# Shaping the decoder's weights and bias inside the first block of a recurrent network with routed experts, and doing both halves of the first projection in a row

## What is computed

```python
xn = layernorm(x)
# branch 1: a recurrence over 2048 steps
x_sub = xn[:, ::2]; x_sub = x_sub * rsqrt(mean(x_sub**2) + eps) * g_norm
x_proj, gate = split(x_sub @ w_in.T + b_in)
h = tanh(h * A + x_proj[t][:, :, None] * Bm)      # for each step t, (4, 512, 64)
y = h @ Cm.sum(0) + Dv * x_proj[t]
s = (y * silu(gate)) @ w_out.T + b_out            # each row used twice
# branch 2: 8 experts, top 2
spikes = sigmoid(xn @ W_enc + b_enc); cont = spikes @ W_s2c + b_s2c
gate8 = normalized top-2 of softmax(cont @ Wr + br)
e_out = sum over experts of gate8 * (relu(cont @ W1 + b1) @ W2 + b2)
decoded = sigmoid(e_out @ W_c2s + b_c2s) @ W_dec + b_dec
g = silu(layernorm(decoded) * ln_g + ln_b)
out = x + s * g
```

## Time and profile before

| | |
|---|---|
| median of 3 runs | 5803.54 us (5798.73 to 5804.52) |
| profiled execution, own time | 5802.78 us |
| its span | 5801.0 us |
| PE busy | 5580.6 us (96%) |
| DVE busy | 5403.5 us (93%) |
| POOL busy | 5287.9 us (91%) |
| ACT busy | 4595.4 us (79%) |

### The profile page before, as it was taken

How to read it: one execution, slowest core, us unless ns; L and a number is a source line. 1 busy time by engine, 2 the same in 40 slices (tenths; PEclk the granted TensorE clock), 3 DMA queues, 4 the chain that set the end, 5 groups by cost and what they waited for, 6 DMA issues and landing times.

```text
span 5801.0 us, 88242 instructions
## 1 busy us (share of the span) xinstructions
PE 5580.6 (96%) x28770; PEld 3073.1 (53%) x28770; DVE 5403.5 (93%) x9108; ACT 4595.4 (79%) x9941; POOL 5287.9 (91%) x2828
## 2 busy tenths in 40 slices
PE   6999999999999999999999999999999999999998
PEld 3555555555555555555555555555555555555554
DVE  5999999999999999999999999999999999999997
ACT  5878878788788787887887878878878788788786
POOL 5999999999999999999999999999999999999997
PEclk9999999999999999999999999999999999999999
DMA  6454544544444445444454454444444444444443
GB/s 166 113 121 107 122 115 111 123 112 116 120 108 121 116 111 122 112 116 120 108 120 117 110 121 113 115 120 109 119 118 110 120 114 114 120 110 118 119 109 88
DMA packets 158222, 673.41 MB, mean 116 GB/s; under 512 B 45761, under 2 KB 46785, under 8 KB 92225
## 3 DMA queue, kind: packets, MB, share of 16 engines
q1 hardware_dynamic: 157762, 667.76, 48.0%
HBM read 617.26 MB, written 50.33 MB: 115 GB/s over the span
## 4 chain that ended last, share of the span: by engine, by line
PE 76%; ACT 14%; DVE 7%; issue 3%; SPq 1%; DMA 0%; POOL 0%; ACTq 0%; POOLq 0%
PE bank L973 17%; PE bank L921 15%; PE ps_y L887 11%; PE ps_acc L985 9%; PE bank L1037 8%; PE ps_acc L1037 8%; ACT h L598 4%; PE bank L908 4%; DVE ps_z L1144 4%; ACT conte L707 3%; DVE ps_z L1138 2%; ACT wide L718 1%; PE bank L1020 1%; PE ps_acc L1020 1%; PE bank L959 1%
## 5 line engine op out<-in xcount | busy, mean ns | idle before, releaser
L525 POOL TENSOR_TENSOR u<-xb,bt 128x1024 f32<-128x1024 f32 x2048 | 4811.0, 2360 | 387.1 <-DVE ps_z L1144 315.6
L598 ACT ACTIVATE h<-ps_z 128x512 f32<-128x512 f32 x4096 | 2408.0, 599 | 1008.3 <-DVE ps_z L1144 807.9
L1138 DVE TENSOR_TENSOR ps_z<-h,ps_A 128x512 f32<-128x512 f32 x4096 | 2664.7, 691 | 314.7 <-ACT h L598 233.1
L1144 DVE TENSOR_TENSOR ps_z<-ps_z,u 128x512 f32<-128x512 f32 x4096 | 2655.3, 691 | 0.0
L973 PE MATMUL bank<-wide,w 65*128 65x256 f32 x4096 | 1015.0, 393 | 18.5 <-ACT wide L718 18.5
L887 PE MATMUL ps_y<-h,c_wide 128*32 128x512 f32 x8192 | 962.0, 599 | 49.0 <-ACT h L598 49.0
L921 PE MATMUL bank<-xnT,w_enc 128*128 128x256 f32 x4096 | 901.3, 381 | 2.8 <-ACT wide L671 2.8
L973 PEld LDWEIGHTS bank<-wide,w 65*128 65x128 f32 x4096 | 730.6, 189 | 315.3 <-issue 152.6
L921 PEld LDWEIGHTS bank<-xnT,w_enc 128*128 128x128 f32 x4096 | 772.9, 190 | 158.9 <-issue 53.3
L887 PEld LDWEIGHTS ps_y<-h,c_wide 128*32 128x32 f32 x8192 | 227.2, 109 | 566.8 <-issue 418.1
L908 PE MATMUL bank<-w_in,xnT 128*128 128x512 f32 x1024 | 474.4, 606 | 7.6 <-DVE c_wide L1214 1.6
(11 more groups left out here) (124 smaller groups left out, 4285.1 us busy)
## 6 DMA issues: line engine op xcount, KB each, us to landing
xb<-x_proj_scratch SPq DMA_DIRECT2D x2048, 256.0 KB, 4.6
xbuf<-in_L_attn_x SPq DMA_DIRECT2D x256, 128.0 KB
xres<-in_L_attn_x SPq DMA_DIRECT2D x512, 64.0 KB
out<-g SPq DMA_DIRECT2D x256, 128.0 KB
x_proj_scratch<-xp SPq DMA_DIRECT2D x256, 64.0 KB
w_in<-in_L_attn_w_in SPq DMA_DIRECT2D x1, 2048.0 KB, 8.1
w_enc<-in_L_ffn_W_enc SPq DMA_DIRECT2D x1, 2048.0 KB, 16.5
w_dec<-in_L_ffn_W_dec SPq DMA_DIRECT2D x1, 2048.0 KB, 20.4
```

Of the source, the lines that this page charges most:

```text
L525: pool.tensor_tensor(u[:, tau % 2, :, :], xt, bt[:, :, :], ALU.mult).then_inc(u_ready, 1)
L598: act.activation(h[:, tau % RING, f, :], ps_z[:, f, :], ACT.Tanh).then_inc(h_ready, 1)
L1138: dve.tensor_tensor(ps_z[:, f, :], h[:, (tau - 1) % RING, f, :], ps_A[:, f, :], ALU.mult).then_inc(m_done, 1)
L1144: dve.tensor_tensor(ps_z[:, f, :], ps_z[:, f, :], u[:, tau % 2, f, :], ALU.add).then_inc(z_ready, 1)
```

## The change

The preamble is shortened. PE sums the columns of the weights as they are loaded; the factor of one half goes into the instructions that use the sums. Both `proj_in` groups run one after the other, and `gt` is made right after `xp`. The eight pieces of `w_dec` (and the small shift) move from the preamble into block 0 on ACT, at the slots 7.5, 8.5, ... 14.5. The bias `b_dec_all` takes four DVE instructions in block 0 in place of three in the preamble, at the slots 3, 4, 5 and 6. On DVE the long reduction for `w_dec_sum` comes behind the short ones for the router. New waits: the first decoding waits for the shaped weights, block 0's two seeds wait for steps of the bias, and in every block but the first `spikes` of bank 0 also waits until the second decoding of the block before is filled.

```diff
+ACT_SHAPE = (7.5, 8.5, 9.5, 10.5, 11.5, 12.5, 13.5, 14.5)
+DVE_SHAPE = (3.0, 4.0, 5.0, 6.0)
...
                 wait_filled(act, at)
+                if k == 0 and not is_first(blk):
+                    wait_dec_filled(act, blk - 1, 1)
                 drained(half_tanhs(bank[k % 2], k, b_enc_col), at)
...
+                if is_first(blk):
+                    act.wait_ge(biases_steps, 4)
                 act.activation(dec_out[q][:, :], b_dec_all[:, :], ACT.Copy).then_inc(dec_seeded, 1)
...
-                if not is_first(blk):
+                if is_first(blk):
+                    act.wait_ge(biases_steps, 1)
+                else:
                     wait_dec_drained(act, blk - 1, 1)
...
             proj_out(0, 0, 0)
+            proj_out(0, 0, 1)
             act.wait_ge(early_loaded, EARLY)
...
+            act.wait_ge(columns_summed, 1)
+            act.activation(cont_bias[0:M, :], ps_y[0:M, 0:1], ACT.Identity, scale=0.5, bias=cont_bias[0:M, :]
+                           ).then_inc(biases_shifted, 1)
+            act.activation(w_s2c[:, :, :], w_s2c[:, :, :], ACT.Copy, scale=0.5)
...
-            act.wait_ge(weights_shaped, 2)
-            for k in range(KH):
-                ins = act.activation(w_dec[:, k, :], w_dec[:, k, :], ACT.Identity, bias=w_dec_shift[:, k:k + 1], scale=0.5)
-            ins.then_inc(weights_shaped, 1)
...
-            proj_out(0, 0, 1)
+            def shape_decoder(k):
+                if k == 0:
+                    act.wait_ge(weights_shaped, 1)
+                    act.activation(w_dec_shift[:, :], w_dec_sum[:, :], ACT.Copy, scale=-0.5 / D).then_inc(weights_shaped, 1)
+                    act.wait_ge(weights_shaped, 2)
+                    act.wait_ge(columns_summed, 2)
+                ins = act.activation(w_dec[:, k, :], w_dec[:, k, :], ACT.Identity, bias=w_dec_shift[:, k:k + 1], scale=0.5)
+                if k == KH - 1:
+                    ins.then_inc(decoder_shaped, 1)
...
             proj_in(0, 0, 0)
-            pe.wait_ge(weights_shaped, 3)
+            proj_in(0, 0, 1)
+            pe.wait_ge(early_loaded, EARLY)
...
+            def shape_bias(n):
+                if n == 0:
+                    dve.wait_ge(columns_summed, 2)
+                    ins = dve.scalar_tensor_tensor(out=b_dec_all[:, :], in0=ps_acc[:, :], scalar=0.5, in1=b_dec_all[:, :],
+                                                   op0=ALU.mult, op1=ALU.add)
+                else:
+                    dve.wait_ge(biases_steps, n)
+                if n == 1:
+                    ins = dve.tensor_reduce(b_dec_sum[:, :], b_dec_all[:, :], AX.X, ALU.add)
+                if n == 2:
+                    ins = dve.tensor_scalar(b_dec_sum[:, :], b_dec_sum[:, :], -1.0 / D, None, ALU.mult)
+                if n == 3:
+                    ins = dve.tensor_scalar(b_dec_all[:, :], b_dec_all[:, :], b_dec_sum[:, :], None, ALU.add)
+                ins.then_inc(biases_steps, 1)
```

More of the change, by code:

```diff
@@ L246, in build @@
         columns_summed = sem("columns_summed")
+        decoder_shaped = sem("decoder_shaped")
         biases_shifted = sem("biases_shifted")
@@ L791, in _ @@
                 act.activation(w_r[rows, E * E:E * E + M], ident[rows, rows], ACT.Copy)
[L792 to L797, removed]
-            act.wait_ge(weights_shaped, 2)
-            for k in range(KH):
-                ins = act.activation(w_dec[:, k, :], w_dec[:, k, :], ACT.Identity, bias=w_dec_shift[:, k:k + 1], scale=0.5)
-            ins.then_inc(weights_shaped, 1)
-            act.wait_ge(columns_summed, 1)
-            act.activation(cont_bias[0:M, :], ps_y[0:M, 0:1], ACT.Identity, bias=cont_bias[0:M, :]).then_inc(biases_shifted, 1)
-            act.wait_ge(biases_shifted, 2)
+            act.wait_ge(biases_shifted, 1)
             act.activation(acc_row[0:M, 0:T2], acc_row[0:M, 0:T2], ACT.Identity, bias=cont_bias[0:M, :]).then_inc(acc_shaped, 1)
             act.wait_ge(acc_shaped, 1)
-            proj_out(0, 0, 1)
+            def shape_decoder(k):
[7 more added lines that the diff above has]
+                    ins.then_inc(decoder_shaped, 1)
             def between(blk, par, slot):
+                for k in range(KH):
+                    if slot == ACT_SHAPE[k]:
+                        if is_first(blk):
+                            shape_decoder(k)
                 if slot == ACT_PROJ_NORM:
@@ L1027, in decode @@
             def decode(blk, q):
+                if is_first(blk) and q == 0:
+                    pe.wait_ge(decoder_shaped, 1)
                 pe.wait_ge(dec_seeded, 2 * blk + q + 1)
@@ L1094, in between @@
                     if slot == PE_PROJ_IN[half]:
-                        proj_in(blk, par, half)
+                        if not is_first(blk):
+                            proj_in(blk, par, half)
                 for n in range(4):
@@ L1217, in _ @@
             dve.wait_ge(early_loaded, EARLY)
-            dve.tensor_reduce(w_dec_sum[:, :], w_dec[:, :, :], AX.X, ALU.add).then_inc(weights_shaped, 1)
             given = w_r[:, E * E:E * E + E]
@@ L1226, in _ @@
                                   br_all[:, :].unsqueeze(1).to_broadcast([P, E, E]),
-                                  br_all[:, :].unsqueeze(2).to_broadcast([P, E, E]), ALU.subtract)
-            dve.tensor_reduce(b_dec_sum[:, :], b_dec_all[:, :], AX.X, ALU.add).then_inc(biases_steps, 1)
-            dve.wait_ge(biases_steps, 1)
-            dve.tensor_scalar(b_dec_sum[:, :], b_dec_sum[:, :], -1.0 / D, None, ALU.mult).then_inc(biases_steps, 1)
-            dve.wait_ge(biases_steps, 2)
-            dve.wait_ge(columns_summed, 1)
-            dve.scalar_tensor_tensor(out=b_dec_all[:, :], in0=ps_acc[:, :], scalar=b_dec_sum[:, :], in1=b_dec_all[:, :],
-                                     op0=ALU.add, op1=ALU.add).then_inc(biases_shifted, 1)
+                                  br_all[:, :].unsqueeze(2).to_broadcast([P, E, E]), ALU.subtract).then_inc(leads_made, 1)
+            dve.tensor_reduce(w_dec_sum[:, :], w_dec[:, :, :], AX.X, ALU.add).then_inc(weights_shaped, 1)
+            def shape_bias(n):
[12 more added lines that the diff above has]
+                ins.then_inc(biases_steps, 1)
             dve.wait_ge(ready, 2)
             def between(blk, par, slot):
+                for n in range(4):
+                    if slot == DVE_SHAPE[n]:
+                        if is_first(blk):
+                            shape_bias(n)
                 for n in range(6):
```

10 lines of the change are left out of this document (7 added, 3 removed).

## The result

The changed kernel takes 5817.69 us (median of 22 runs, 5802.53 to 5847.4), the kernel before in the same series 5804.47 us. The ratio is 1.0019, 95% interval [1.001, 1.0028]: 11 us slower (the two medians are 13.2 us apart), at the edge of what can be told from no change. The forecast was 5807 with a range to 5813, so the time lies outside it.

The account below looks back on a forecast made before the run. The prediction took PE's chain, handed from first expert to first expert, as the bound, so block 0's shift counts once: -1.9 + 0.9 + 1.3 + 3.7 = +4.0 us, giving 5807 us, range 5801 to 5813.

Parts of the forecast that it names:

- Only the start is moved, the lag is handed on once: Whole kernel: PE's shift at block 0's first expert changes the total once, not 64 times; the 89.17 us period stays.
- -1.9, the lead lost behind POOL's wait: Block 0's scan: of 18 us gained in the preamble, 1.9 are left at step 1, as POOL waits for `dv_all`.
- +0.9, the bias on DVE: Block 0, slots 3 to 6: four operations cost 1.7 us, slack hides part, net 0.8 to 0.9; bounds 0 and 2.7.
- +1.3, the low clock in two fills: Block 0's last two encoder fills, after PE's gap: 1.2 GHz loses 2.75 us, turning a 1.0 lead into 0.3 lag.
- +3.7, the pieces on ACT: Block 0, slots 7.5 to 14.5: `w_dec` pieces of 0.62 us each delay the experts by 3.7 us; bounds 0 and 5.0.
- The extra wait costs nothing: `spikes` of bank 0 in 63 blocks: handling the added wait costs nothing while below ACT's slack of about 0.2 us.
- The sum, +4.0: Whole kernel: -1.9 + 0.9 + 1.3 + 3.7 gives 4.0 us slower, forecast 5807; chance 72%, own range 5803 to 5811.
- If L553 comes earlier: Sign for block 0: POOL's L553 stays near 65.8 us behind `dv_all`; if it came earlier, the prediction would be wrong.
- The clock is the larger loss: Block 0: fills lose 7.2 us instead of 2.75, a 1.2 GHz stretch at first experts 1.5; +10, 5813 us; chance 10%.

## Why the prediction was wrong

- **Only the start is moved, the lag is handed on once.** Right: 195.04 in both profiles, the period unchanged.
- **-1.9, the lead lost behind POOL's wait.** Right in size. From the landing of `dv_all` to step 1's sum it was 71.27 - 65.76 = 5.51 us and is 65.52 - 61.92 = 3.60: 1.91 gained. Incomplete in cause: I named one wait, and taking it away moved the scan to the next two on the same queue of loads.
- **+0.9, the bias on DVE.** Mis-sized. The four cost 0.68 + 0.68 + 0.15 + 1.20 = 2.71, and the slack meant to cover 0.9 was not there: one wait for ACT of 0.92 remained. ACT was late there because its `spikes` ahead of that tanh had waited 0.85 us for PE's slow fill, so the low clock took the slack away. From step 1's sum to step 7's the scan now takes 84.08 - 65.52 = 18.56 us, against 87.38 - 71.27 = 16.11: 2.45 later. The fourth operation took 1.20 while POOL was in a `u`, and 0.49 in the kernel with the pieces in idle time, where POOL stood still. The total did not show this, since ACT's last `spikes`, which follows PE, was where the sum had it.
- **+1.3, the low clock in two fills.** Right: 9.88 against 7.17 is 2.71, forecast 2.75; with the 3.84 taken off, the last `spikes` has a lag of 0.32, forecast 0.3.
- **+3.7, the pieces on ACT.** Right: from 0.32 to 3.84 is 3.5. Moving them behind the experts gave back 2.7 at the first expert.
- **The extra wait costs nothing.** Right, and without it the time is the same. The Trainium skill ("Advanced Engine Details and Errata", Miscellaneous Facts) has 50 to 100 ns for reading a semaphore; the 6 us that I had worked out from it, were it on the chain, are not there.
- **The sum, +4.0.** It holds for undisturbed executions: 5806.7 and 5806.4 against 5802.8 to 5804.0, some +3, and 3.84 in the trace. Its signs hold with the 3.84 of luck added: step 1's sum 69.36, first expert 109.11. One of them was badly chosen: "If L553 comes earlier" came true, at 61.92, though nothing in its mechanism had changed. In the nine profiles with `fin_skip` behind the late loads and the shorter preamble it begins anywhere from 61.92 to 69.90.

The step that failed is the price of TensorE's clock. The sum has a term for it only in the two fills, and nothing for the experts; a clock that falls there stands only in the rival "The clock is the larger loss". That rival had the place, "one more stretch at 1.2 GHz among the first experts", and even the cause, "as ACT's delay opens gaps there", but priced it by the 1.46 us that the `y` matmuls had lost in a short stretch, at a chance of 10%. At the experts, of block 0 or in the loop, the clock does not return after a few us: it stays down through the experts' matmuls (weights of 65x128 and 128x64) and costs 13 to 16 us. I had taken for granted that what the clock costs is what the one execution in hand shows; its profile had no fall in the loop, while in 22% of the executions of the same kernel there was one. The change made that two in three, so the median moved from the lowest step into the next: 5817.7 - 5806.7 = 11.0 us. The means tell the same: 5817.4 against 5806.1 over the 22 runs of each, and 5806.9 against 5803.4 over the undisturbed ones, so some 3.5 us come from the lag and some 8 from the falls.

The Trainium skill ("TensorE: Matmul & The Clock Gate", Part 1) advises for modelling to count the ramp as under 1% of a kernel. The trace agrees: the clock of 0.994 means that all stretches at the low clock together cost the profiled execution at most 0.6%. But the 13 us of one fall are 0.2% of 5812 us, and that is all there was to forecast here. The same part ties the half clock to idle time of PE. Block 18 shows PE busy for 27 us at 0.50, and in the 5 us before it PE was busy for 4.71 at 1.00; here the measurement goes against the rule.

Shown: the pieces of work on ACT at these slots of block 0 make the falls frequent, in the kernel before as in the changed one; the added wait and PE's long gap do not. Open: why. PE's wait ahead of the first expert goes with it (1.04 to 1.42 us where falls are common, 0.80 and 1.15 in between, 0.34 where they are rare), but filling it or taking out its piece left 5 of 12. A rival was not tested: PE's wait for `xbuf` of the second block, where the shorter stretch at 0.50 begins. It is 2.76 us before the change, 3.28 to 3.69 in the four profiles with a fall at block 0's experts, and 2.55 to 3.68 in the seven others that keep the loads in their order, so its length alone does not decide. Nor is it known what a delay in block 0 has to do with falls 18 blocks later, or whether it has anything to do with them.

## What to carry to other kernels

List the executions one by one beside their granted clock before a forecast: where they come in steps, forecast the lag of a step and the share of each step separately, because a median jumps when the share passes one half. Work of an engine that idles goes into its idle time (here the 16 us in which DVE, and ACT behind it, waited for `u` of step 1), not into the steps where the critical chain runs along that engine, even when its sum is only 3 us. A wait that ends an idle time is a floor only until the next one: before counting on a lead, follow the whole queue of loads behind it.

## What the runs showed of the hardware

- TensorE's clock fell from 1.00 to 0.50 some 0.4 to 5 us after the start of a block's experts, in the loop always 4.50 or 4.51 us after it, while PE went from one expert matmul to the next, and came back 27 to 34 us later, when most of them were done. With a wholly unchanged program this happens in one execution and not in the next.
- In the kernel with the dummy matmuls 3.35 us without work, after 18 us of dense matmuls at 1.00, were followed by a clock of 0.50.
- One DMA issue behind the load of `w_2` held SP's queue for 15.93 us (10.28 us in the kernel before).
- The same DVE operation on 128x512 in place took 1.20 us beside a running POOL operation and 0.49 us with POOL idle.
